# Dealing out anew the block sums that a graph kernel begins in its first layer, with unread matmuls in one step

## The reference

```python
h = relu(layernorm(x))
x = x + L0(h, U, Dmat, head_w, edges)   # attention over edges, 4 heads of rank 16,
                                        # softmax per target, then a dense proximal step
h = relu(layernorm(x))                  # the rows called h2 below
msg = h[src] + relvectors[edge_type]
red = segment_sum(msg, dst)             # second layer: sum over a node's edges
x = x + gru_cell(red, h, w_ih, w_hh, b_ih, b_hh)
```

## Time and profile before

| | us |
|---|---|
| median of three timed executions | 971.59 |
| lowest and highest of them | 970.59, 977.33 |
| the profiled execution | 978.19 |
| span in its profile | 976.4 |
| TensorE, VectorE, ScalarE, GpSimd busy in it | 858.0, 637.5, 418.0, 648.1 |
| mean granted TensorE clock, as a share of full speed | 0.85 |

### The profile page before, as it was taken

One profiled execution on the slowest core, in us unless ns is written; L12 is line 12 of the kernel. 1 busy time (PEld: TensorE's weight loads), 2 busy tenths in 40 slices (PEclk: granted clock), 3 DMA queues, 4 the chain that ended last, 5 costly groups with the idle time before them and its releaser, 6 DMA issues.

```text
span 976.4 us, 15073 instructions
## 1 busy us (share of the span) xinstructions
PE 858.0 (88%) x5101; PEld 690.2 (71%) x5101; DVE 637.5 (65%) x1329; ACT 418.0 (43%) x811; POOL 648.1 (66%) x975
## 2 busy tenths in 40 slices
PE   5955797769988988999999998999988999999795
PEld 5845585556767887877788876888875666666473
DVE  5353677676776759677976785777754354556853
ACT  5522345543554546454665544555522221111241
POOL 4598988888888888888888888888860011111000
PEclk9955658785676669678999997999968999999998
DMA  9355133444444444454555554455542465555210
GB/s 201 71 124 161 55 68 96 129 124 123 99 135 99 111 116 128 130 127 121 142 153 155 147 143 111 117 150 153 139 109 64 123 189 147 156 160 177 74 37 21
DMA packets 59396, 119.20 MB, mean 122 GB/s; under 512 B 16593, under 2 KB 36751, under 8 KB 56189
## 3 DMA queue, kind: packets, MB, share of 16 engines
q1 hardware_dynamic: 39810, 93.29, 30.2%
q0 software_dynamic: 18448, 24.82, 15.7%
q10 hardware_dynamic: 1056, 0.07, 0.1%
HBM read 81.34 MB, written 36.68 MB: 121 GB/s over the span
## 4 chain that ended last, share of the span: by engine, by line
POOL 49%; PE 32%; issue 7%; DVE 7%; DMA 3%; SPq 1%; ACT 1%; DVEq 0%; ACTq 0%; POOLq 0%
POOL shared L836 25%; POOL cnt_rows L841 13%; POOL zs_third L836 11%; PE bank L2285 7%; PE bank L2315 4%; PE bank L2117 4%; PE bank L2284 3%; PE bank L2170 3%; PE bank L2037 2%; PE bank L2316 2%; DVE zus L1113 2%; DMA shared<-zu_table,src_col 1%; PE bank L2202 1%; PE bank L1940 1%; PE bank L2220 1%
## 5 line engine op out<-in xcount | busy, mean ns | idle before, releaser
L836 POOL DMA_INDIRECT shared<-zu_table,src_col x306 | 297.4, 972 | 52.1 <-issue 49.2
L841 POOL MEMSET cnt_rows<- 54x300 f32 x450 | 165.2, 367 | 0.3
L836 POOL DMA_INDIRECT zs_third<-zu_table,src_col x144 | 140.9, 978 | 23.2 <-issue 23.2
L2037 PEld LDWEIGHTS bank<-zus,shared 125*128 125x128 f32 x900 | 139.1, 247 | 16.8 <-issue 13.1
L2037 PE MATMUL bank<-zus,shared 125*128 125x64 f32 x900 | 141.4, 333 | 7.4 <-ACT setup L1803 3.0
L2170 PE MATMUL bank<-layer,oh 128*125 128x84 f32 x900 | 136.0, 325 | 0.8 <-DVE layer L1199 0.8
L2170 PEld LDWEIGHTS bank<-layer,oh 128*125 128x125 f32 x900 | 133.3, 240 | 1.1 <-issue 1.1
L1113 DVE TENSOR_TENSOR setup<-iota_b,bank 128x500 bf16<-128x500 bf16 (+1 forms) x224 | 124.5, 609 | 8.0 <-PE bank L2242 7.8
L1746 ACT ACTIVATE shared<-shared,node_id 125x2304 f32<-125x2304 int32 x25 | 55.4, 2216 | 97.5 <-PE bank L2037 59.0
L859 POOL DMA_DIRECT2D shared<-counts_table x22 | 11.7, 535 | 101.9 <-PE bank L2285 90.9
L1803 ACT ACTIVATE setup<-bank 125x500 bf16<-125x500 f32 (+1 forms) x91 | 57.3, 680 | 49.7 <-PE bank L2242 48.4
(11 more groups left out here) (254 smaller groups left out, 1700.4 us busy)
## 6 DMA issues: line engine op xcount, KB each, us to landing
shared<-in_edges SPq DMA_DIRECT2D x25, 1125.0 KB
own_table<-own_out SPq DMA_DIRECT2D x25, 375.0 KB
counts_table<-setup SPq DMA_DIRECT2D x13, 683.6 KB
shared<-own_table SPq DMA_DIRECT2D x14, 448.0 KB
counts_table<-cnt_rows SPq DMA_DIRECT2D x9, 683.6 KB
shared<-zu_table,src_col POOLq DMA_INDIRECT x306, 3.8
zs_third<-own_table SPq DMA_DIRECT2D x7, 448.0 KB
h_table<-h2s SPq DMA_DIRECT2D x25, 125.0 KB
```

The source lines that it names most:

```text
L836: nc.gpsimd.indirect_dma_start(out=zs[t % 3][:, j * KR:(j + 1) * KR], out_offset=None, in_=zu_table, in_offset=bass.IndirectOffsetOnAxis(a ...
L841: nc.gpsimd.memset(idle[t >= FIRST], 0.0).then_inc(idle_set, 1)
L2037: last = mm(ps(c, 128, (j - a) * KR, (j - a + 1) * KR), ohT[:, j * 128:(j + 1) * 128], zus[0:W, t, :], start=True, stop=True)
```

## The change

The table that says which group is begun when and from where is dealt out anew. `FOLLOW` goes from 7 to 13: groups 0 to 12 are now all begun from reloaded counts, in steps 9 to 21 in the order 1 to 6, 0, 7 to 12, each over `min(step - 1, 14)` blocks. Groups 13 to 20 are begun in step t+2 from the staging buffer as before, over `min(t + 1, 18)` blocks, of which 14 stand early in the step (18 for groups 19 and 20) and the rest late. The choice of staging buffer stays as it was (`TURNS`). Reloaded parts are summed in the other half of bank 5 (`part_sums`), so a part waits only for the copy of the last part in its own half (`parts_before`). A step may now have two last parts; ScalarE copies both out in the next step, one behind the other, and SyncE stores both. In step 22 TensorE issues 21 matmuls of `iota_b` with itself, 250 columns each, into a part of bank 2 that nothing reads (`keep_clock`), ahead of count group 6.

```diff
@@ tables
-        FOLLOW = 7
+        FOLLOW = 13
+        TURNS = 7
+        LARGEST = 18
         MOST = 14
         SINGLE = 19
-        AGAIN = {15 + n: t for n, t in enumerate((1, 2, 3, 4, 5, 6, 0))}
+        AGAIN = {9 + n: t for n, t in enumerate((1, 2, 3, 4, 5, 6, 0, 7, 8, 9, 10, 11, 12))}
+        STEP_OF = {t: step for step, t in AGAIN.items()}
         def second_buffer(t):
-            return t >= FOLLOW and t % 2 == 1 or t >= SINGLE
+            return t >= TURNS and t % 2 == 1 or t >= SINGLE
         def begun(t):
-            return 0 if t not in PARTS else min(t + 1, MOST) if t >= FOLLOW else MOST
+            return 0 if t not in PARTS else min(t + 1, LARGEST) if t >= FOLLOW else min(STEP_OF[t] - 1, MOST)
         def early_blocks(t):
-            return MOST if t + 2 in AGAIN or t >= SINGLE else MOST // 2
+            return LARGEST if t >= SINGLE else MOST
         def middle_part(t):
-            return t - 2 if t - 2 in PARTS[FOLLOW:] and early_blocks(t - 2) == MOST else None
-        def last_part(t):
-            return AGAIN[t] if t in AGAIN else t - 2 if t - 2 in PARTS[FOLLOW:] and middle_part(t) is None else None
+            return t - 2 if t - 2 in PARTS[FOLLOW:] and begun(t - 2) <= early_blocks(t - 2) else None
+        def last_parts(t):
+            follows = [t - 2] if t - 2 in PARTS[FOLLOW:] and middle_part(t) is None else []
+            reloaded = [AGAIN[t]] if t in AGAIN else []
+            return follows + reloaded
+        def part_sums(t):
+            return ps(5, W, D, 2 * D) if t < FOLLOW else ps(5, W, 0, D)
+        def parts_before(t):
+            same = [p for p in PART_ORDER[:nth_part(t) - 1] if (p < FOLLOW) == (t < FOLLOW)]
+            return nth_part(same[-1]) if same else 0
@@ SyncE, prefetch; ScalarE does the same with keep_part
-                if last_part(t - 1) is not None:
-                    store_part(last_part(t - 1))
+                for n in last_parts(t - 1):
+                    store_part(n)
@@ ScalarE, keep_part
-                nc.scalar.activation(part_out(t), ps(5, W, 0, D), ACT.Copy).then_inc(part_kept, 1)
+                nc.scalar.activation(part_out(t), part_sums(t), ACT.Copy).then_inc(part_kept, 1)
@@ TensorE, end of attend
-                begin_sum(t - 2, early_blocks(t - 2), MOST)
+                begin_sum(t - 2, early_blocks(t - 2), LARGEST)
                 if t in AGAIN:
                     begin_sum_again(t)
                 if counts:
                     count_ahead(t - 1, 5)
+                if t == AHEAD:
+                    keep_clock(7)
+                if counts:
                     count_ahead(t - 1, 6)
+            def keep_clock(blocks):
+                for n in range(3 * blocks):
+                    mm(ps(2, W, D, D + 2 * W).rearrange("p (a w) -> p a w", a=2), iota_b[:, :],
+                       iota_b[:, :].unsqueeze(1).broadcast_to([128, 2, W]), start=True, stop=True)
@@ TensorE, begin_sum
-                    if nth_part(t) > 1:
-                        pe.wait_ge(part_kept, nth_part(t) - 1)
+                    if parts_before(t):
+                        pe.wait_ge(part_kept, parts_before(t))
@@ TensorE, begin_sum_again
                 pe.wait_ge(l_again, AGAIN_BASE + 32 * (step - min(AGAIN) + 1))
-                pe.wait_ge(part_kept, nth_part(t) - 1)
-                part_blocks(t, again, 0, MOST)
+                pe.wait_ge(last_third, begun(t))
+                pe.wait_ge(a_col, 3 * len(GROUPS))
+                if parts_before(t):
+                    pe.wait_ge(part_kept, parts_before(t))
+                part_blocks(t, again, 0, begun(t))
@@ TensorE, part_blocks
-                        last = mm(ps(5, W, 0, D), counts[:, a * W:(a + 1) * W], thirds(a)[:, m, :],
+                        last = mm(part_sums(t), counts[:, a * W:(a + 1) * W], thirds(a)[:, m, :],
                                   start=a == 0 and m == 0, stop=a == begun(t) - 1 and m == 2)
```

More of the change, by code:

```diff
@@ L264, in begun @@
         def begun(t):
-            return 0 if t not in PARTS else min(t + 1, MOST) if t >= FOLLOW else MOST
+            return 0 if t not in PARTS else min(t + 1, LARGEST) if t >= FOLLOW else min(STEP_OF[t] - 1, MOST)
         def early_blocks(t):
-            return MOST if t + 2 in AGAIN or t >= SINGLE else MOST // 2
+            return LARGEST if t >= SINGLE else MOST
         def middle_part(t):
-            return t - 2 if t - 2 in PARTS[FOLLOW:] and early_blocks(t - 2) == MOST else None
-        def last_part(t):
-            return AGAIN[t] if t in AGAIN else t - 2 if t - 2 in PARTS[FOLLOW:] and middle_part(t) is None else None
-        PART_ORDER = [p for t in range(NW) for p in (middle_part(t), last_part(t)) if p is not None]
+            return t - 2 if t - 2 in PARTS[FOLLOW:] and begun(t - 2) <= early_blocks(t - 2) else None
[3 more added lines that the diff above has]
+            return follows + reloaded
+        PART_ORDER = [p for t in range(NW) for p in [middle_part(t)] + last_parts(t) if p is not None]
+        assert sorted(PART_ORDER) == list(PARTS)
         def nth_part(t):
             return PART_ORDER.index(t) + 1
+        def part_sums(t):
[3 more added lines that the diff above has]
+            return nth_part(same[-1]) if same else 0
         def part_out(t):
@@ L1697, in attend @@
                 cuts(t + 1, 1 - h)
-                if last_part(t - 1) is not None:
-                    keep_part(last_part(t - 1))
+                for n in last_parts(t - 1):
+                    keep_part(n)
                 if t >= 2:
```

## The result

| us | before | after |
|---|---|---|
| median of the timed executions, same chip | 976.34 (20 runs, 967.60 to 979.86) | 971.17 (20 runs, 964.71 to 980.62) |
| profiled execution, its span | 978.19, 976.4 | 977.25, 975.3 |

The ratio of the times is 0.9953, with an interval from 0.9932 to 0.9974. The change gains 4.6 us (2.5 to 6.6), where 10.45 us were forecast. One of the 20 executions after (980.62 us) counts as slow and is left out of the ratio, which is therefore not that of the two medians.

What follows compares the result with a forecast made beforehand. Three limits were said to take turns: gathers, TensorE at full clock, and TensorE after its clock fell. Terms -5.95 + 6.2 - 10.7 = -10.45 us gave 967.7 on the profiled execution, 961 on the median, range 954 to 974.

Steps and rivals of the forecast that it cites:

- forecast sum of +0.25 us: Dealing of begun blocks over both layers: -5.95 us in the second layer and +6.2 us in the first.
- Part 4: Unread products in step 22: cost 0 inside a 2.31 us wait, keep step 23's clock, gain 10.7 us (0 to 13.7).
- rival A: Step 23: products don't save the clock, or it wasn't lost in the timed runs; 971.8 us, chance 0.23.
- the logits that need it come near 735 even then: Step 23: last gather out by about 724 us, so its logits come near 735 even with the clock kept.
- The limit of the first layer: First layer: from 597.72 us TensorE never waits for a gather and is the chain until step 23.
- Part 3: First layer, steps 18 to 22: 19 added blocks on TensorE without slack cost 6.2 us (3 to 12).
- Part 2: Second layer: 22 blocks fewer bring 7.15 us, 1.2 of it lost in the steps of groups 17 to 20.
- Part 5: Steps 9 to 14, sums from reloaded counts: falls behind steps 10 and likely 11 go, no time gained or lost.
- B: Step 18 keeps its clock: 4.0 us more gained, 957.1 us, less up to 2 more; chance 0.16.
- C: Steps 9 to 14: filler taken from the middle lets the clock fall; 979.8 us, chance 0.07.

Runs made afterwards that it cites:

- e1: The changed kernel without the 21 unread products in step 22, against the kernel before: 976.49 us, ratio 0.9991.
- e2: The kernel before with the 21 unread products alone, at the same place in step 22: 972.03 us, ratio 0.9950.
- e16: The kernel before, memsets kept, with unread products ahead of count group 5 in steps 2 to 12 and 22, run again: 969.52 us, ratio 0.9955.
- e8: The kernel before without the memsets behind the gathers, unread products ahead of count group 5 in step 22: 947.91 us, ratio 0.9710.
- e10: The kernel before without memsets behind the gathers, unread products ahead of count group 5 in steps 2 to 12 and 22: 920.87 us, ratio 0.9458.
- e6: The kernel before with the 21 unread products ahead of count group 5 in step 22: 971.24 us, ratio 0.9942.
- e14: The kernel before without memsets, unread products in steps 2 to 12 and 22, run again on another chip: 924.02 us, ratio 0.9477.
- e15: The changed kernel without memsets, unread products ahead of count group 5 in steps 2 to 8 and 22, against the kernel before: 942.03 us, ratio 0.9676.
- e3: The changed kernel with the 21 unread products moved ahead of count group 5, against the kernel before: 969.42 us, ratio 0.9942.
- e4: The changed kernel with 12 fewer begun blocks (at most 16 a group, 14 for groups 19 and 20), against the kernel before: 972.47 us, ratio 0.9959.
- e12: The changed kernel without memsets, unread products in steps 2 to 8 and 22, on the chip of 1044.14 us: 1306.34 us, ratio 1.2554.
- e13: The kernel before, memsets kept, unread products in steps 2 to 12 and 22, on the chip of 1044.14 us: 1040.04 us, ratio 0.9986.

## Why the prediction was wrong

In one sentence: the dealing came out near its forecast sum of +0.25 us (e1: ratio 0.9991) though both of its terms were mis-sized, and the products brought about half of the 10.7 that the forecast gave them (e2: ratio 0.9950, 4.9 us).

**Part 4, the 10.7 us.** This is the step that failed. What happens in step 23 was right: its head runs at the full clock, e1 shows it lost without the products, and from that head to the edge sums of step 24 the kernel after takes 9.6 us less and e2 10.0 us less. Two things make 4.9 of it. First, "The wait they stand in is 2.31 us, so they cost 0" was a misreading. The row of 713.95 is a run of five products, four of count group 5 and one of group 6, and the wait stands ahead of group 5. The products come behind it and cost 2.3 us in e2, 3.34 in the kernel after. In e2's trace 8.0 us are left of the 10.0 at the edge sums of step 24 (738.03 against 745.99), and 7.4 of the time (970.78 against 978.19). Second, "I apply the difference to the median": the term was read off one execution of 978.19 us and taken off the median of the timed ones. But 8 of 20 executions of the kernel before end by 972.4 us without any products, about as early as those of e2. If the products take 8 us off the long ones only, 12 of 20, that makes 4.8 us, an estimate that meets the 4.9. That the short executions are those that keep the clock in step 23 is likely and not shown, since no trace holds one; it would be the second half of rival A, "or it wasn't lost in the timed runs".

The prediction's own caution, "the logits that need it come near 735 even then", was no bound: in e2 they come at 733.48 and in e16 at 726.99, released by TensorE's and ScalarE's work in step 23 and not by the last gather.

The rule of the Trainium skill, page "TensorE: Matmul & The Clock Gate", section "Part 1: The HAM clock gate", that for modelling the ramp costs under 1% of a typical span, was set aside in the prediction. The rule speaks of one ramp, and for the one fall that the products remove the measurement agrees with it: 0.5%. For the falls of steps 2 to 12 it doesn't once the gathers are fast: from e8 (ratio 0.9710) to e10 (0.9458) lie 2.5% of the time.

**The limit of the first layer.** "From 597.72 on TensorE never waits for a gather again, and until step 23 it is the chain" is right of that one trace: its chain leaves GpSimd at 593 us. What was wrong is to build on it that TensorE has no slack. TensorE was catching up on a delay of its own (the fall in step 18), at 25.8 us a step against the gathers' 27, and by step 22 it had just caught up: its logits stand at 704.75, and in e2, where TensorE waits for the gathers, at 704.65. In e2 and e6, where step 18 keeps its clock, steps 19 to 21 take 26.8 to 27.4 us with waits for gathers, and the chain runs through GpSimd until about 700 us. What was missing is one more look: the row of the last gather, and that no idle time of that queue is a wait for a buffer. e16 and e14 show what hangs on the queue: 45.5 us between memsets and none.

**Part 3, "+6.2", no slack.** The blocks have that price where TensorE sets the pace: e15 against e14 shows 7.3 for 22. Beside the gathers the dealing moved the head of step 23 by 2.8 us (718.8 in e3, 716.0 in e6), and e1 shows no time that can be measured. The lower bound, 3 us "if those steps come to wait for gathers anyway", was the right end.

**Part 2, "1.2" lost.** It was 3.9: 7.15 less the 3.3 of e3 (196.70 against 199.99, neither with a fall), nearer to the other bound of 5.2. "Long filler" and short copies, the reason for 0.3 a step, missed the loop through VectorE, ScalarE's queue and the gates: two blocks fewer, 7 instead of 9, bring 0.15 us a step and not 0.65 (e4). In the profiled execution of the kernel after a fall of the clock took 1.65 us more.

**Part 5** had the end right, since nothing came of steps 9 to 14, and the steps wrong. The falls behind steps 10 and 11 did go: the heads of steps 11 and 12 take 4.20 us. But TensorE met the gathers already at step 11, and the forecast had no fall of the clock behind those waits. Ahead of L2057 TensorE waited 6.87 and 2.63 us, not "up to 1 us", and the clock fell there: steps 11 and 12 were to take 22 to 27 us and took 30.4 and 28.3. Step 15 began at 503.5, 2.5 us later, within the slack of 4.2.

**The rivals.** A's time, 971.8, lies near the measured 971.17, but it counts from 971.59 and forecasts no gain; counted from the median of 20 it would be 976.6. The products did save the clock. B (step 18 keeps its clock) happened in these traces, 26.8 us against 32.7. In e1 step 19 begins 4.4 us sooner by it (610.0 against 614.4), and the added blocks of steps 19 to 22 take it back (106.8 us against 101.9). C, filler taken from the middle, can't be read from the kernel after: steps 11 and 12 lost the clock behind waits for gathers, but so did step 13 of e2, with the old dealing (a wait of 4.79 us, and 28.0 us for the step). Without the memsets steps 9 to 14 of e15 take 16.7 us more than those of e14, though e15 had come to the head of step 9 earlier by 7.7 (328.1 against 335.8).

## What to carry to other kernels

Before pricing anything on the busiest engine, look for a queue that never waits: if its idle times are all issue, it sets a pace that the others can only meet, and what is saved elsewhere counts only behind its last instructions. Check by its waits whether the tail behind it hangs on it at all. When the times of a kernel fall into two groups, find out which of them the traced execution belongs to before taking its microseconds off the median. Filler that is to hold the clock is cheaper ahead of the instruction that waits (the head of step 23 came 2.8 us sooner in e3's trace, though the times don't settle it), and a run of equal instructions in a timeline may join two calls, so count them before placing it. A block of work moved between stages costs its full price where it goes if its engine sets the pace there, and returns it only down to the next loop.

## What was not expected of the hardware

- A memset of 54x300 elements behind each gather takes 0.37 us, 450 times. Leaving it out shortens the pace by less, from 1.47 us between two starts (719.58 to 721.05 before) to 1.25 (641.91 to 643.16 in e14), because the issue time ahead of a gather grows from 0.16 to 0.30 us; the gather itself stays at 0.97 to 0.98 us. Even so 45.5 us of the whole time hang on it once TensorE keeps up (e14 against e16).
- The same pair of waits (0.93 and 1.68 us in step 23) was followed by edge sums of 7.70 us in the kernel after and of 4.13 us in e3: the length of a wait doesn't tell whether the clock falls.
- The same kernel took 1044.14 us on one chip and 971 to 978 us on the others. The kernel of e12 lost there 26% against it, and gained 3% as e15 elsewhere. On that chip TensorE waited by issue for 101.6 us ahead of its edge sums in e12, but for some 17 us in all in e13, and GpSimd's issue time ahead of a gather in e12 was the 0.3 us of the other kernels without memsets. What disturbed it stays open.
